# Role-conditioned adapter with layer norm: the first batch's weights picked on chip, finer first loads, and another order of VectorE's first up phase

## What is computed

```python
h = jnp.einsum('bsh,bhk->bsk', hidden_states, W_down[role]) + b_down[role][:, None, :]
h = jax.nn.gelu(h, approximate=False)
u = jnp.einsum('bsk,bkh->bsh', h, W_up[role]) + b_up[role][:, None, :]
y = hidden_states + u
mean = jnp.mean(y, axis=-1, keepdims=True)
var = jnp.mean(jnp.square(y - mean), axis=-1, keepdims=True)
yn = (y - mean) * jax.lax.rsqrt(var + LN_EPS)
return yn * gamma[role][:, None, :] + beta[role][:, None, :]
```

## Time and profile before

| what | us |
|---|---|
| median of three runs | 365.76 |
| lowest and highest | 365.07, 366.26 |
| the profiled execution's own time | 365.14 |
| its span, first to last instruction | 363.3 |
| TensorE busy | 353.4 (97%) |
| VectorE busy | 288.5 (79%) |
| ScalarE busy | 185.5 (51%) |
| chain that ended last: TensorE's share | 96% |

### The profile page before, as it was taken

The page is one execution under the profiler, slowest core; times in us unless marked ns, Lnnn a source line. Parts: engine busy times, 40 slices in busy tenths (PEclk is TensorE's granted clock), DMA queues, the critical chain, the costliest instruction groups (busy, mean ns, idle before and its releaser), DMA issues.

```text
span 363.3 us, 4947 instructions
## 1 busy us (share of the span) xinstructions
PE 353.4 (97%) x1548; PEld 289.5 (80%) x1548; DVE 288.5 (79%) x296; ACT 185.5 (51%) x295; POOL 40.5 (11%) x73
## 2 busy tenths in 40 slices
PE   6999999999999999999999999999999999999992
PEld 2888888878888888888888888888888888888881
DVE  2897989897896878968798787986789777873476
ACT  4793566762646626564375623656346571615131
POOL 0000221003200112002110021100301002200012
PEclk9999999999999999999999999999999999999997
DMA  7999999989777887789757896696958911570023
GB/s 206 405 390 412 410 411 399 316 298 380 281 258 290 251 327 256 237 302 327 299 196 236 299 357 262 235 362 184 391 166 267 359 58 66 222 258 32 0 115 116
DMA packets 27227, 96.59 MB, mean 266 GB/s; under 512 B 3154, under 2 KB 3410, under 8 KB 27218
## 3 DMA queue, kind: packets, MB, share of 16 engines
q1 hardware_dynamic: 23040, 81.80, 63.2%
q10 hardware_dynamic: 4178, 14.69, 10.2%
HBM read 79.70 MB, written 16.78 MB: 266 GB/s over the span
## 4 chain that ended last, share of the span: by engine, by line
PE 96%; DMA 2%; DVE 1%; SPq 0%; issue 0%; ACT 0%; DVEq 0%
PE up_ps L275 48%; PE down_ps L268 48%; DMA wd_stage<-W_down 1%; DVE h_full L573 0%; DMA roles_sb<-roles 0%; DVE rows L579 0%; DVE up_ps L556 0%; SPq L149 0%; ACT wd_hi L461 0%; SPq L238 0%; DVEq L42 0%; DVE last_mean L566 0%; DVE neg_shift L564 0%; SPq L239 0%; DVEq L555 0%
## 5 line engine op out<-in xcount | busy, mean ns | idle before, releaser
L268 PE MATMUL down_ps<-x_hi,wd_hi 128*128 128x512 f32 x256 | 81.8, 390 | 1.7 <-ACT wd_hi L459 0.9
L268 PE MATMUL down_ps<-x_hi,wd_lo 128*128 128x512 f32 x256 | 81.4, 389 | 0.0
L268 PE MATMUL down_ps<-x_lo,wd_hi 128*128 128x512 f32 x256 | 81.4, 389 | 0.0
L275 PE MATMUL up_ps<-wu_hi,h_hi 128*128 128x512 f32 x256 | 79.6, 389 | 0.1
L275 PE MATMUL up_ps<-wu_hi,h_lo 128*128 128x512 f32 x256 | 79.5, 389 | 0.0
L275 PE MATMUL up_ps<-wu_lo,h_hi 128*128 128x512 f32 x256 | 79.4, 389 | 0.0
L268 PEld LDWEIGHTS down_ps<-x_hi,wd_hi 128*128 128x128 f32 x256 | 47.9, 188 | 12.5 <-issue 2.6
L275 PEld LDWEIGHTS up_ps<-wu_hi,h_hi 128*128 128x128 f32 x256 | 47.9, 188 | 10.5 <-issue 0.5
L275 PEld LDWEIGHTS up_ps<-wu_lo,h_hi 128*128 128x128 f32 x256 | 48.1, 188 | 10.0
L268 PEld LDWEIGHTS down_ps<-x_lo,wd_hi 128*128 128x128 f32 x256 | 48.0, 188 | 10.0
L275 PEld LDWEIGHTS up_ps<-wu_hi,h_lo 128*128 128x128 f32 x256 | 48.0, 188 | 10.0
(11 more groups left out here) (46 smaller groups left out, 253.3 us busy)
## 6 DMA issues: line engine op xcount, KB each, us to landing
wu_stage<-W_up SPq DMA_DIRECT2D x32, 512.0 KB, 7.3
rows<-x SPq DMA_DIRECT2D x32, 512.0 KB, 4.1
x_stage<-xT SPq DMA_DIRECT2D x31, 512.0 KB, 8.4
wd_stage<-W_down SPq DMA_DIRECT2D x31, 512.0 KB, 8.8
out<-rows ACTq DMA_DIRECT2D x28, 512.0 KB, 4.7
b_up_row<-b_up SPq DMA_DIRECT2D x8, 512.0 KB, 3.6
gamma_row<-gamma SPq DMA_DIRECT2D x8, 512.0 KB, 6.4
beta_row<-beta SPq DMA_DIRECT2D x8, 512.0 KB, 7.3
```

Of the source, the lines that this page charges most:

```text
L268: return pe.matmul(down_ps[:, kc, :], wd_part[:, n, c * K + kc * P:c * K + (kc + 1) * P], x_part[:, n, c * S:(c + 1) * S], start=start, st ...
L275: mm = pe.matmul(up_ps[:, t % 2, half], h_part[:, kc, t * P:(t + 1) * P], wu_part[:, kc, half], start=(kc == 0 and h_part is h_hi and wu_p ...
```

## The change

**The head.** Between the loads of x's two first chunks, SP now loads the first 256 columns of W_down's chunk 0 for all three roles (`early_wd`, 384 KB in runs of 1 KB, into the tile `rows`, row tile 0, which is free then). VectorE reads the role itself and copies the role's 256 columns into `wd_hi`; the rest of the chunk (128 KB) comes by role as before. TensorE runs the first two kc tiles of chunk 0 through all three passes on these columns, then the other two. Parts 0 and 1 of x and W_down are loaded, rounded, split and multiplied in chunks of 256 KB. The load of b_down goes behind ScalarE's rounding of part 1. Eleven warm-up matmuls stand in place of 12.

**The down phase of batch 0.** Part 2 is multiplied whole, all four kc, and only part 3 goes kc by kc.

**ScalarE, batch 0.** All four `gelu` come ahead of the rounding of batch 1's part 0; before, that rounding stood behind the first one.

**VectorE, batch 0's up phase.** The order is written anew.

The core of the diff:

```diff
-    WARM_UP = 12
+    WARM_UP = 11
+    EARLY = K // 2
+        early_wd = rows[:, 0, 0:R * EARLY]
...
             def load_rows(b, t):
                 if not is_first(b):
                     sp.wait_ge(stored[t], 16 * b)
+                elif t == 0:
+                    sp.wait_ge(early_wd_lo, 1)
...
+            load_first_x(0, 0, first_x_landed[0])
+            sp.dma_start(early_wd.rearrange("p (r k) -> p r k", r=R),
+                         W_down.rearrange("r (p n) k -> p n r k", p=P)[:, 0, :, 0:EARLY]).then_inc(early_wd_landed, 16)
+            load_first_x(0, 1, x_landed[0])
             sp.wait_ge(roles_landed, 16)
             first_role = load_role(sp, 0)
+            load_first_wd(0, 0, first_wd_landed[0], skip=EARLY)
+            load_first_wd(0, 1, wd_landed[0])
+            load_first_x(1, 0, first_x_landed[1])
+            load_first_wd(1, 0, first_wd_landed[1])
+            load_first_x(1, 1, x_landed[1])
+            load_first_wd(1, 1, wd_landed[1])
+            for i in range(2, NLOAD):
                 load_x_part(0, i)
                 load_wd_part(first_role, i)
...
+            def first_chunk():
+                pe.wait_ge(first_x_hi, 1)
+                for early in (True, False):
+                    kcs = range(KC // 2) if early else range(KC // 2, KC)
+                    for down_pass in range(len(PASSES)):
+                        if down_pass == 0:
+                            pe.wait_ge(early_wd_hi if early else first_wd_hi, 1)
+                        elif down_pass == 1:
+                            pe.wait_ge(first_x_lo, 1)
+                        else:
+                            pe.wait_ge(early_wd_lo if early else first_wd_lo, 1)
+                        for kc in kcs:
+                            down(0, 0, kc, down_pass, start=(down_pass == 0))
...
+                if first:
+                    pe.wait_ge(x_split, NLOAD - 1)
+                    pe.wait_ge(wd_split, NLOAD - 1)
+                    for kc in range(KC):
+                        for c in range(CPL):
+                            for down_pass in range(len(PASSES)):
+                                down(NLOAD - 2, c, kc, down_pass)
                 for kc in range(KC):
-                    for n in range(NLOAD // 2, NLOAD):
+                    for n in range(NLOAD - 1 if first else NLOAD // 2, NLOAD):
...
-                gelu(0, 0, role)
+                for kc in range(KC):
+                    gelu(0, kc, role)
                 round_next_part(0, 0)
-                gelu(0, 1, role)
-                gelu(0, 2, role)
-                gelu(0, 3, role)
                 round_next_part(0, 1)
                 variance(0, 0)
...
+            def split_first_part():
+                dve.wait_ge(roles_landed, 16)
+                own = early_wd[:, bass.ds(load_role(dve, 0) * EARLY, EARLY)]
+                dve.wait_ge(early_wd_landed, 16)
+                dve.tensor_copy(wd_hi[:, 0, 0:EARLY], own).then_inc(early_wd_hi, 1)
+                split_first(x_lo, x_stage, x_hi, 0, slice(0, S), first_x_hi, first_x_lo)
+                dve.wait_ge(early_wd_hi, 1)
+                dve.tensor_tensor(wd_lo[:, 0, 0:EARLY], own, wd_hi[:, 0, 0:EARLY].bitcast(F32),
+                                  ALU.subtract).then_inc(early_wd_lo, 1)
...
             def first_steps():
                 for i in range(KC):
                     split_wu(0, i)
-                split_h(0, 0)
+                for kc in range(KC):
+                    split_h(0, kc)
+                bias_tile(0, 0)
+                bias_tile(0, 1)
+                sum_tile(0, 0)
                 split_x_part(1, 0)
                 split_wd_part(1, 0)
-                split_h(0, 1)
-                split_h(0, 2)
-                split_h(0, 3)
-                for t in range(NT):
-                    bias_tile(0, t)
-                sum_tile(0, 0)
+                bias_tile(0, 2)
+                centre_tile(0, 0)
+                sum_tile(0, 1)
+                finish_tile(0, 0)
                 split_x_part(1, 1)
                 split_wd_part(1, 1)
-                centre_tile(0, 0)
-                finish_tile(0, 0)
+                bias_tile(0, 3)
+                centre_tile(0, 1)
+                sum_tile(0, 2)
+                finish_tile(0, 1)
                 split_x_part(1, 2)
-                sum_tile(0, 1)
                 split_wd_part(1, 2)
-                centre_tile(0, 1)
-                split_x_part(1, 3)
-                finish_tile(0, 1)
-                sum_tile(0, 2)
-                split_wd_part(1, 3)
                 centre_tile(0, 2)
                 finish_tile(0, 2)
+                split_x_part(1, 3)
+                split_wd_part(1, 3)
```

More of the change, by code:

```diff
@@ L102, in bass_role_adapter_layernorm @@
         wd_landed = [sem(f"wd_landed{i}") for i in range(NLOAD)]
-        first_x_landed = sem("first_x_landed")
-        first_wd_landed = sem("first_wd_landed")
+        first_x_landed = [sem(f"first_x_landed{i}") for i in range(NLOAD // 2)]
+        first_wd_landed = [sem(f"first_wd_landed{i}") for i in range(NLOAD // 2)]
+        early_wd_landed = sem("early_wd_landed")
         wu_landed = [sem(f"wu_landed{i}") for i in range(KC)]
@@ L112, in bass_role_adapter_layernorm @@
         first_x_hi = sem("first_x_hi")
+        first_x_lo = sem("first_x_lo")
+        early_wd_hi = sem("early_wd_hi")
+        early_wd_lo = sem("early_wd_lo")
         first_wd_hi = sem("first_wd_hi")
+        first_wd_lo = sem("first_wd_lo")
         wu_hi_ready = sem("wu_hi_ready")
@@ L278, in up, with chunk @@
                 return mm
+            def first_chunk():
[11 more added lines that the diff above has]
+                            down(0, 0, kc, down_pass, start=(down_pass == 0))
+            def chunk(n, c):
+                for down_pass in range(len(PASSES)):
+                    if down_pass == 0:
+                        pe.wait_ge(x_hi_ready if c else first_x_hi, n + 1)
+                        pe.wait_ge(wd_hi_ready if c else first_wd_hi, n + 1)
+                    elif down_pass == 1:
+                        pe.wait_ge(x_split if c else first_x_lo, n + 1)
+                    else:
+                        pe.wait_ge(wd_split if c else first_wd_lo, n + 1)
+                    for kc in range(KC):
+                        mm = down(n, c, kc, down_pass)
+                return mm
             def steps(b):
@@ L285, in steps @@
                     parts = NLOAD * b + n + 1
-                    chunks_apart = first and n == 0
+                    if first:
+                        if n == 0:
+                            first_chunk()
+                        else:
+                            chunk(n, 0)
+                        mm = chunk(n, 1)
+                        mm.then_inc(d_part_used, 1)
+                        continue
                     for down_pass in range(len(PASSES)):
-                        if down_pass == 0 and not chunks_apart:
+                        if down_pass == 0:
                             pe.wait_ge(x_hi_ready, parts)
@@ L295, in steps @@
                         for c in range(CPL):
-                            if chunks_apart and down_pass == 0:
-                                pe.wait_ge(*((first_x_hi, 1) if c == 0 else (x_hi_ready, 1)))
-                                pe.wait_ge(*((first_wd_hi, 1) if c == 0 else (wd_hi_ready, 1)))
                             for kc in range(KC):
@@ L349, in round_wd_part, with round_first @@
                 act.copy(wd_hi[:, i, :], wd_stage[:, i, :]).then_inc(wd_hi_ready, 1)
+            def round_first(hi, stage, i, chunk, landed, ready):
+                act.wait_ge(landed, 16)
+                act.copy(hi[:, i, chunk], stage[:, i, chunk]).then_inc(ready, 1)
             def round_next_x(b, i):
@@ L450, in _ @@
             act.dma_start(roles_sb[:, :], roles).then_inc(roles_landed, 16)
-            act.dma_start(b_down_all[:, :], b_down_cols).then_inc(b_down_landed, 16)
             act.wait_ge(constants_ready, 2)
             act.activation(unused[:, :], eps[:, :], ACT.Gelu)
[L454 to L462, removed]
+            round_first(x_hi, x_stage, 0, slice(0, S), first_x_landed[0], first_x_hi)
+            round_first(x_hi, x_stage, 0, slice(S, CPL * S), x_landed[0], x_hi_ready)
+            round_first(wd_hi, wd_stage, 0, slice(EARLY, K), first_wd_landed[0], first_wd_hi)
+            round_first(wd_hi, wd_stage, 0, slice(K, CPL * K), wd_landed[0], wd_hi_ready)
+            round_first(x_hi, x_stage, 1, slice(0, S), first_x_landed[1], first_x_hi)
+            round_first(wd_hi, wd_stage, 1, slice(0, K), first_wd_landed[1], first_wd_hi)
+            round_first(x_hi, x_stage, 1, slice(S, CPL * S), x_landed[1], x_hi_ready)
+            round_first(wd_hi, wd_stage, 1, slice(K, CPL * K), wd_landed[1], wd_hi_ready)
+            act.dma_start(b_down_all[:, :], b_down_cols).then_inc(b_down_landed, 16)
+            for i in range(2, NLOAD):
                 round_x_part(0, i)
```

(16 more changed lines are left out.)

12 lines of the change are left out of this document (7 added, 5 removed).

## The result

The changed kernel takes 368.73 us (median of 19 runs, 367.34 to 370.74) beside 365.52 for the kernel before (19 runs). The measured ratio is 1.009, with a 95% interval of 1.007 to 1.0109: **slower by 0.9%, or 3.2 us**. I had forecast slower, 367.2 us, with a range that ended at 368.4. The profiled execution took 369.13 us, with a span of 367.3, 4.0 more than before.

What follows compares the result with a forecast made beforehand. TensorE was taken as bound by VectorE's zero margin at split_h(1, 3). The head's 1.36 us gain is lost waiting and TensorE ends 1.46 late: 365.14 + 1.46 = 366.6, plus 0.62 gives 367.2 us; range 364.9 to 368.4.

Steps and rivals of the forecast that it cites:

- where the kernel is bound: At 77.21 us TensorE needs split_h(1, 3), where VectorE's margin is nil; arriving earlier gains only if VectorE is earlier too.
- the head: Start of the kernel: early columns of W_down let TensorE start at about 5.5 us, gaining 1.36 us (0.7 to 1.7).
- VectorE's new order: Batch 0's up phase: finish of tile 0 at 41.84, sum_tile(0, 3) at 56.96 instead of 55.50, 1.46 us later.
- the chain: Batch 0's last sum delays tile 2's store, then batch 1's rows 2, bias and splits; TensorE goes on 1.46 us late.
- the same distances: Store of batch 0's tile 2 to batch 1's bias: 10.65 us kept from before, so 58.69 gives bias at 69.34.
- the step that left the late load of b_up at nothing: bias_tile(0, 3) at 46.5 instead of 36.35 delays b_up and eight loads; queue dry 1 to 2 us, priced at nothing.
- The third rival: Dry queue bites: batch 1's rows 2 another 1 to 2 us later, bias 71, median 368.3 to 368.9; chance 0.16.
- the 0.62 us between median and profiled execution: Whole kernel: the median of the runs lies 0.62 above the profiled execution, turning 366.6 into 367.2.
- the forecast's case: Batch 1's up phase: TensorE waits 1.7 us before the first block, 2.8 in all over four pieces; chance 0.50.
- the clock: TensorE's waits before batch 1's up blocks stay under the 2.6 us or so through which the clock stayed at 1.00.
- The rule on a load's time: Store of tile 2: the rule's 3.2 us would mean no wait for rows 2 and 365.7; set aside for 6.9 traced.

Runs made afterwards that it cites:

- Experiment 3: Changed kernel with VectorE's and ScalarE's orders of batch 0's up phase as in the kernel before; 365.33 us, ratio 0.9984.
- experiment 8: Changed kernel with the old VectorE and ScalarE orders, bias_tile(b, 2) behind the splits of h, and sum_tile(0, 1) ahead of split_x_part(1, 2); 363.98 us, ratio 0.9951.
- experiment 10: Changed kernel, new orders kept, with batch 2's parts 0 and 1 loaded ahead of b_up and bias_tile(b, 2) behind the splits of h; 363.60 us, ratio 0.9929.
- experiment 1: Changed kernel with SP loading batch 2's parts 0 and 1 ahead of b_up in batch 0; 367.33 us, ratio 1.0028.
- experiment 2: Changed kernel with bias_tile(0, 3) moved directly behind bias_tile(0, 2) on VectorE; 367.13 us, ratio 1.0036.
- experiment 11: The changed kernel itself, run again beside the kernel before; 369.34 us, ratio 1.0076.
- experiment 12: Changed kernel with TensorE's wait before batch 1's up phase filled by 14 matmuls on zeros; 369.00 us, ratio 1.0074.
- experiment 9: Kernel before with only two VectorE moves: bias_tile(b, 2) behind the splits of h, and batch 0's sum_tile(0, 1) one place earlier; 365.52 us, ratio 0.9993.
- experiment 7: Changed kernel with the old VectorE and ScalarE orders in batch 0 and bias_tile(b, 2) behind the four splits of h; 364.83 us, ratio 0.9985.
- experiment 4: Kernel before with only the new VectorE and ScalarE orders of batch 0's up phase; 371.54 us, ratio 1.0139, four runs.
- experiment 6: Changed kernel with bias_tile(b, 2) moved behind the four splits of h in every batch; 366.43 us, ratio 1.0027.

## Why the prediction was wrong, point by point

**Right: where the kernel is bound.** TensorE without margin at `split_h(1, 3)`, so that a gain of the head alone is lost. Experiment 3 shows just that (nothing gained), and experiments 8 and 10 that the gain returns when VectorE is given room.

**Right: the head,** 1.22 us measured where I took 1.36. First down matmul at 5.77 (I took 5.3 to 5.9); the early columns landed by 5.33, for which I had 5.0; chunk 1 of W_down was rounded from 8.30 on, as I had it.

**Nearly right: VectorE's new order.** I had it at the finish of tile 0 at 41.84 after a wait of 1.1 us. It started at 40.84 without one, 2.88 us after the start of ScalarE's variance instead of the 4.04 of the earlier trace rows. GpSimd's two operations for that factor took 0.32 and 0.55 us where before they took 0.73 and 1.48; why isn't known. `sum_tile(0, 3)` was at 56.13 instead of my 56.96, still 0.63 later than before.

**Right: the chain, but not its length.** Sum, store, rows 2, bias, splits. The store went out at 57.87 and the bias of its rows began at 71.42. From store to bias I had kept "the same distances", 10.65 us; it was 13.55, and 11.40 in experiment 1 with the queue fed.

**Wrong: the step that left the late load of b_up at nothing** ("only the rows behind them can suffer; I leave this at nothing and keep 2 us for the range"). I had b_up's issue nearly right (46.5, measured 45.69) and named the rows behind it, and still priced it at zero for the forecast and let the queue be dry for "1 to 2 us". It moved 1.3 MB too little, which is 3.2 us, and the rows of tiles 0 and 1, which I had on time, were 3.2 and 4.1 us later than before. The forecast of 367.2 fell 1.5 us short, and feeding the queue gave back 1.4 us in experiment 1 and 1.6 in experiment 2: that is about the size of the term I had left at nothing. The third rival, chance 0.16, was the case: it had rows 2 biased at 71, where 71.42 was measured, and a median of 368.3 to 368.9, which holds the measured 368.73. My range cut it in half at 368.4. That its median fits so well is in part luck: without the 0.62 us between median and profiled execution it gives 367.7 to 368.3 for the profiled one, which took 369.13. What I had for the forecast's case, a wait of 1.7 us before the first up block, is what the profile of experiment 1 shows once the queue is fed.

**Wrong, but small: the clock.** I said that the waits would stay short of what makes the clock fall. The longest was 3.76 us instead of 1.7, and the clock fell. It cost 0.3 us by the medians of experiments 11 and 12 and 0.45 by the rows of the up phase.

**The rule on a load's time.** The Trainium skill, page "DMA: Bandwidth & Descriptors", section "Anatomy of one DMA — SWDGE (gpsimd) path", has 2.0 us plus bytes over 436 GB/s, an estimate of 3.2 us for 512 KB. The store here took 7.32 us and the rows behind it 6.07, with other loads in the queue. Where the queue was fed earlier the trace agrees: the same load of rows took 3.3 us in the profiles of experiments 1 and 2. For the full queue the measurement decides, and there the rule gives too little.

**Open.** Experiment 1's median lies 1.3 us above its profiled execution, and the changed kernel's runs spread over 3 us, while those of experiments 8 and 10 spread over 1.2 and 1.4. A stretch at half clock in most of experiment 1's runs, as their mean clocks suggest, would be part of it; no profile shows it. The kernel before spreads too: 24 of its 104 executions beside all these runs took more than 367.2 us, most of these with a mean granted clock of 0.985 to 0.991. So did 4 of 12 in experiment 9, which also has the old head, but none of the 42 in experiments 3, 7, 8 and 10, which have the new one. The stall in the old head in experiment 4's profile (a wait of 2.7 us, and half clock behind it) may be what one sees there. If so, the new head does more than its 1.2 us in the profile, but no profile of such an execution of the kernel before is there to show it.

## What to carry to other kernels

When an instruction is moved in an order written by hand, ask which load its result releases, and then what stands behind that load in the same queue: here one bias tile, 9 us later, held back b_up and four loads behind it, and the damage showed 20 us on in another batch. A side effect named in words but priced at zero belongs in the sum, worked out in bytes not moved. And before shortening the head of a pipeline whose second engine has no margin, make the margin first: the two small moves of experiments 1 and 6 turned 0.9% slower into 0.7% faster.

## What the runs showed of the hardware that I had not expected

**After the gap the queue didn't come back at its full rate.** In the changed kernel from 47 us on, with loads issued again, the DMA engines were busy but moved far less than the 411 GB/s of the full queue:

```profile
47.00:49.00 2.00, 2.00 (x10) 1.65 (x10) 2.00 (x4) 1.10 (x3) 0.00 (x0) 1.00 0.97 231
...
51.00:53.00 2.00, 2.00 (x11) 1.65 (x10) 1.87 (x3) 0.35 (x1) 0.74 (x1) 1.00 0.91 190
```

A share of 0.97 with 231 GB/s, against 1.03 with 411, means 1.7 times the busy time for each byte. The second profile of the changed kernel (experiment 11) has 207 GB/s from 46 to 54 us, and experiment 6, with b_up as late, 298. Why is open. In these rows the share of busy DMA engines doesn't tell that a queue is well fed, the GB/s do.

**The clock fell after a wait of 2.15 us** (experiment 2, 0.50 from 76 to 78 us) but not in the kernel with a wait of 1.7 us (experiment 1, 1.00 throughout), and in the kernel before it was still at 1.00 in the 2.6 us behind the last matmul. The length of the wait alone didn't decide it in these three runs.
